# Attention inside a two-layer kernel: probabilities times values in three rounded passes, score rows through ScalarE and GpSimd

## Chip, cores and metric

One Trainium2 chip, one of its cores. The metric is the device time of one execution in microseconds (us), median of several runs.

## The reference

Two sequences of 1024 tokens, width 256. The kernel computes layer norm and attention with residual, a feed-forward layer with ternary weights, a Mamba layer and a feed-forward layer with 2:4 sparsity. Only attention matters here: 16 heads of 128 channels, causal, with a bias that grows linearly with the key position.

```python
q = (resid_pre @ Wq.T).reshape(b, s, H, DH)      # k, v likewise
scores = jnp.einsum('bqhd,bkhd->bhqk', q, k) / math.sqrt(DH)
scores = jnp.clip(scores, -1024.0, 1024.0)
scores = scores + _alibi_mask(H, s, s)[None]
attn = jax.nn.softmax(scores.astype(jnp.float32), axis=-1).astype(q.dtype)
z = jnp.einsum('bhqk,bkhd->bqhd', attn, v)
out = jnp.einsum('bqhd,ohd->bqo', z, Wo.reshape(d, H, DH))
```

## The kernel before

Attention runs as 16 bodies, one per pair of heads: 8 pairs for batch 0, then 8 for batch 1. The five engines have an instruction stream each, written out by hand, and meet at counting semaphores. An engine works its stream strictly in order, so the order in which a stream lists its steps is the order of the work.

Matrix products of fp32 accuracy are done in one of two ways. Most operands are split in a high part, rounded to the format fp32r, and a low part (the difference), and three passes high x high, high x low, low x high go into one accumulator (`passes`, line 265). The product of probabilities and values (`pe_product`, line 501) takes plain fp32 operands, `pt` and `v_sb`, in one instruction, which the trace shows as two records.

A score row k is 128 queries of one head against all keys up to them. Rows 0 to 7 are the first head of the pair, 8 to 15 the second; row k has (k mod 8 + 1) x 128 columns. In the text s12 is the product that computes row 12. A row goes this way: TensorE computes it into PSUM (`pe_scores`, 473); VectorE clips it into the tile `prob` in SBUF (`scores`, 1266), which frees the PSUM bank (`s_read`), then adds the causal bias and takes the row's minimum of the negated values in one custom instruction (1271, called the mask in this text); ScalarE takes the exponential and the row sum (`exps`, 892); VectorE the reciprocal (`recip`, 1277); GpSimd multiplies (`norm`, 1769). Then TensorE transposes 128 x 128 blocks of it.

The body has 24 slots. Slot n does the transposes of value block n (`pe_transposes`, up to four), then one larger job, `USES[n]`, then the product of block n-1. The larger jobs are in this order:

```python
USES = ("v1", "s12", "s13", "out1", "s8", "qk0", "s9", "s10", "s11", "qk1", "s14", "s15",
        "qk2", "s4", "s5", "qk3", "s0", "s1", "s2", "s3", "s6", "v0", "s7", "out0")
```

v1 and v0 project values (v0 those of the next pair), qk0 to qk3 project queries and keys of the next pair, out1 and out0 are output projections. Rows from s4 on in this list are already those of the next pair. The larger jobs use two double banks of PSUM in turn: a job in slot n needs that the result of slot n-2 has been read (`pe_free`, 418). A result is read by whoever evacuates it: scores by VectorE's clip, qk by ScalarE (high half) and then VectorE (low half), v by ScalarE (884) alone, out by VectorE's residual (1289). A transposed block is in one of two further banks and copied by ScalarE (`pts`, 899) into `pt`, which also has two buffers. The accumulators of the product are two more banks; they are read by ScalarE (`z`, 904) and VectorE (`z_rest`, 1282). Per pair there are 12 blocks of 512 columns, and 4 each of 384, 256 and 128.

Beside that, each body prepares a slice of the ternary weights on VectorE: `q_start` (1295), the four small steps `q_scales` (1319 to 1325), `q_signs` (1329, 1330) and the four bf16 steps `q_values` (1335 to 1342), 512 columns wide in batch 0, 256 in batch 1. GpSimd computes the low parts of the weights with subtractions from SBUF: `split_qk` (1747, for the pair after the next), `split_v` (1754) and `split_out` (1761), after ScalarE has rounded the high parts (855, 860, 866). Weights come by DMA from the SyncE queue.

VectorE's stream at the end of a body, with `ahead(k)` the clip and mask of row k of the next pair, is: `ahead(3)`, `next_recip(2)`, `ahead(6)`, `next_recip(3)`, `next_recip(6)`, `q_values()`, `ahead(7)`, `residual(out0)`.

Of the kernel before, what the change touches and what calls it, by code (L numbers as in the profile page):

```python
# [8 lines left out]
F32 = mybir.dt.float32  # L9
# [29 lines left out]
def program(nc, x_in, slopes_in, wqk_in, wv_in, wo_in, wgu0_in, wp0_in, win_in, wx_in, wdt_in,  # L39
# [3 lines left out]
    with ctx:  # L43
# [49 lines left out]
        v_sb = place(mem, "v_sb", [P, TILES, 2 * DH])  # L93
# [3 lines left out]
        pt = place(mem, "pt", [P, 2, BANK])  # L97
# [23 lines left out]
        def causal_row(k):  # L121
# [108 lines left out]
         o_added, wv_in_s) = (  # L230
# [4 lines left out]
                "wv_in"))  # L235
# [47 lines left out]
        USES = ("v1", "s12", "s13", "out1", "s8", "qk0", "s9", "s10", "s11", "qk1", "s14", "s15",  # L283
# [10 lines left out]
        def s_count(p, name, last=False):  # L294

            mine = [n for n in USES[:USES.index(name) + 1] if n[0] in "qs" and has(n, False, last)]
            return p * 20 + (FIRST_S + len(mine))

# [119 lines left out]
        def pe_free(pe, p, pos, begin=False, last=False):  # L418
# [4 lines left out]
            if prev == -2:  # L423
                pe.wait_ge(s_read, p * 20 + FIRST_S)
# [4 lines left out]
            elif USES[prev][0] in "qs":  # L429
                pe.wait_ge(s_read, s_count(p, USES[prev], last))  # L430
# [59 lines left out]

        def pe_transposes(pe, p, idx):
# [33 lines left out]
        def pe_attention(pe):  # L525
# [30 lines left out]
            for m in range(4):  # L556
                if m >= 2:
                    pe.wait_ge(s_read, m - 1)
                pe_qk(pe, 0, 0, m, m)
            for i, qt in enumerate(ROWS[:-1]):  # L560
                pe.wait_ge(s_read, 4 + i - 1)
# [3 lines left out]
            pe.wait_ge(s_read, 4 + 6)  # L565
            pe_v(pe, 0, 0, 0, 7)
            pe.wait_ge(s_read, 4 + 7)
# [10 lines left out]
            pe.wait_ge(s_read, s_count(LAST_PAIR, "s15", True))  # L578
# [271 lines left out]
        def act_attention(act):  # L850
# [30 lines left out]
            def v(p, m, pos):  # L881
                act.wait_ge(v_full, p * 2 + (m + 1))
                act.wait_ge(pv_done, p * 24 + (2 if m else 2 - 4))
                nc.scalar.activation(v_sb[:, 4 * m:4 * m + 4, :].rearrange("p t n -> p (t n)"),
                                     ps[:, s_bank(pos):s_bank(pos) + 2, :].rearrange("p a n -> p (a n)"),
                                     ACT.Copy).then_inc(v_read, 1)
# [8 lines left out]
            def pts(p, idx):  # L895
# [3 lines left out]
                nc.scalar.activation(pt[:, idx % 2, r0 * P:BANK], ps[:, 4 + idx % 2, r0 * P:BANK],  # L899
                                     ACT.Copy).then_inc(pt_read, 1)  # L900
# [6 lines left out]
            def body(p, b, begin=False, two_on=True, last=False):  # L907
# [8 lines left out]

                pts(p, 0)
                v(p, 1, 0)
                pts(p, 1)
                if not begin:  # L920
                    z(p - 1, 1, 1)
                pts(p, 2)
                exps(p, 12)
                q_magnitudes(p, b)
                pts(p, 3)
# [1008 lines left out]
```

## Time and profile before

| | |
|---|---|
| median of 3 runs | 1860.01 us (1858.03 to 1860.28) |
| profiled execution | 1858.39 us |
| its span | 1856.6 us |
| TensorE (PE) busy | 1714.1 us, 92% |
| VectorE (DVE) busy | 1415.1 us, 76% |
| ScalarE (ACT) busy | 1127.9 us, 61% |
| GpSimd (POOL) busy | 647.9 us, 35% |
| mean granted clock of TensorE | 0.976 |

The busy shares are means over stages with different limits. Attention lasts from the start to about 1006 us. A record of the timeline gives the start in us from the span's start, the duration, the engine, the line, the operation, the tile written and the tiles read. PE is TensorE's matmul; its records overlap, because matmuls are pipelined, so the time that a matmul takes is the distance from its start to the next one's. A bracket at the end of a line is idle time of that engine before the instruction, and what ended it.

### The profile page before, as it was taken

The numbers are of one execution on the slowest core, as the hardware profiler recorded it, in microseconds if no ns is written. First come the engines' busy times: TensorE is split into PE (matmuls) and PEld (weight loads), VectorE is DVE, ScalarE is ACT, GpSimd is POOL, SyncE is SP. The second block draws the span as 40 slices with busy tenths as digits, with TensorE's granted clock in tenths as the row PEclk, the third lists the DMA queues.
The fourth block names the chain that finished last, engine by engine and source line by source line (L and its number), as shares of the span: only waits on it lengthen the run. The fifth ranks groups of instructions, "written<-read, shape, count | busy, mean of one in ns | idle before, by whom it ended". The sixth has DMA issues, their size and how long they took to land. (4 is left out here: it accounts for less than half of the span.)

```text
span 1856.6 us, 30197 instructions
## 1 busy us (share of the span) xinstructions
PE 1714.1 (92%) x9232; PEld 1318.5 (71%) x9232; DVE 1415.1 (76%) x2239; ACT 1127.9 (61%) x2108; POOL 647.9 (35%) x517
## 2 busy tenths in 40 slices
PE   5999999999999999999998997899899798977997
PEld 3777778877877787778786886655457565556886
DVE  6777777777776777677764667788887788867997
ACT  3555555555555555565554554899877998943332
POOL 2332323322332233232221111089680397870000
PEclk9999999999999999999999998999999899998999
DMA  2000000000000000000001000123110232220000
GB/s 92 18 29 17 23 28 17 17 23 28 15 26 15 23 14 25 14 23 21 13 0 47 0 0 1 36 93 102 68 68 4 70 101 79 97 84 1 11 17 18
DMA packets 24139, 64.03 MB, mean 34 GB/s; under 512 B 2769, under 2 KB 7889, under 8 KB 23697
## 3 DMA queue, kind: packets, MB, share of 16 engines
q1 hardware_dynamic: 24080, 63.31, 10.2%
q8 instruction: 31, 0.51, 0.1%
q14 instruction: 28, 0.22, 0.0%
HBM read 60.94 MB, written 2.36 MB: 34 GB/s over the span
## 5 line engine op out<-in xcount | busy, mean ns | idle before, releaser
L1769 POOL TENSOR_SCALAR prob<-prob,rinv 128x640 f32<-128x640 f32 (+7 forms) x256 | 213.6, 835 | 674.3 <-DVE rinv L1277 673.1
L1846 POOL TENSOR_TENSOR m_h<-m_h,m_C 128x1024 f32<-128x1024 f32 x128 | 305.8, 2392 | 195.0 <-DVE m_h L1656 195.0
L1656 DVE TENSOR_TENSOR_SCAN m_h<-m_y,ps 128x1024 f32<-128x1024 f32 x128 | 291.5, 2284 | 53.9 <-PE ps L765 47.2
L892 ACT ACTIVATE prob<-prob,nmax 128x640 f32<-128x640 f32 (+7 forms) x256 | 198.4, 775 | 192.6 <-DVE nmax L1271 192.5
L508 PE MATMUL ps<-pt,v_sb 128*128 128x512 f32 (+3 forms) x768 | 310.4, 486 | 1.9 <-ACT pt L899 1.9
L899 ACT ACTIVATE pt<-ps 128x512 f32<-128x512 f32 (+3 forms) x384 | 186.1, 485 | 151.2 <-PE ps L498 150.1
L772 PE MATMUL ps<-m_h,ident 128*128 128x512 f32 x512 | 250.0, 612 | 11.3 <-POOL m_h L1846 11.3
L1271 DVE CUSTOM_DVE_ANT_0 prob<-prob,bias 128x640 f32<-128x640 f32 (+7 forms) x256 | 204.4, 799 | 44.8 <-issue 27.5
L498 PEld LDWEIGHTS ps<-ident,prob 128*128 128x128 f32 x1152 | 145.6, 140 | 116.6 <-issue 88.7
L1266 DVE TENSOR_SCALAR prob<-ps 128x640 f32<-128x640 f32 (+7 forms) x256 | 192.4, 751 | 42.4 <-PE ps L479 40.6
L1143 ACT ACTIVATE m_u<-m_uT,m_bT 128x256 f32<-128x256 f32 x512 | 211.1, 502 | 9.2 <-PE ps L765 9.1
L498 PE MATMUL ps<-ident,prob 128*128 128x128 f32 x1152 | 188.4, 273 | 0.0
L765 PEld LDWEIGHTS ps<-ident,m_u 128*128 128x128 f32 x1024 | 122.7, 144 | 90.6 <-issue 53.2
L479 PE MATMUL ps<-qk_hi 128*128 128x512 f32 (+2 forms) x384 | 153.8, 400 | 22.1 <-DVE qk_lo L1257 13.4
L765 PE MATMUL ps<-ident,m_u 128*128 128x128 f32 x1024 | 137.9, 278 | 19.9 <-DVE m_h L1656 8.4
L772 PEld LDWEIGHTS ps<-m_h,ident 128*128 128x128 f32 x512 | 89.6, 195 | 80.8 <-issue 63.9
L1149 ACT ACTIVATE m_y<-m_delta,negA 128x1024 f32<-128x1024 f32 x128 | 139.9, 1143 | 3.0 <-DVE m_h L1656 3.0
L508 PEld LDWEIGHTS ps<-pt,v_sb 128*128 128x128 f32 x768 | 131.7, 189 | 13.2 <-ACT pt L899 3.0
L479 PE MATMUL ps<-qk_hi,qk_lo 128*128 128x512 f32 (+2 forms) x384 | 132.0, 344 | 0.0
L479 PE MATMUL ps<-qk_lo,qk_hi 128*128 128x512 f32 (+2 forms) x384 | 131.7, 343 | 0.0
L1014 ACT ACTIVATE f_sg<-ps 128x512 f32<-128x512 f32 x64 | 38.1, 598 | 134.3 <-PE ps L618 134.3
L479 PEld LDWEIGHTS ps<-qk_hi 128*128 128x128 f32 x384 | 72.8, 190 | 38.3 <-DVE qk_lo L1257 17.3
(210 smaller groups left out, 3485.0 us busy)
## 6 DMA issues: line engine op xcount, KB each, us to landing
m_C<-bc_dram SPq DMA_DIRECT2D x64, 512.0 KB, 3.7
wqk_raw<-wqk_in SPq DMA_DIRECT2D x16, 512.0 KB, 3.3
wv_raw<-wv_in SPq DMA_DIRECT2D x16, 256.0 KB, 2.6
wo_raw<-wo_in SPq DMA_DIRECT2D x16, 256.0 KB, 2.9
x<-x_in SPq DMA_DIRECT2D x2, 1024.0 KB, 6.8
q_raw<-wgu_in SPq DMA_DIRECT2D x8, 256.0 KB, 2.7
raw<-wgu_in SPq DMA_DIRECT2D x1, 2048.0 KB, 7.9
out<-x SPq DMA_DIRECT2D x8, 256.0 KB, 2.1
```

The source lines that it names most:

```text
L479: mm = nc.tensor.matmul(flat[:, o + lo_c:o + hi_c], (qk_hi, qk_lo)[a][:, 2 * u, qt * P:(qt + 1) * P], (qk_hi, qk_lo)[w][:, 2 * u + 1, lo_c ...
L498: mm = nc.tensor.transpose(ps[:, 4 + idx % 2, r * P:(r + 1) * P], prob[:, at:at + P], ident[:, :])
L508: nc.tensor.matmul(ps[:, 6 + g, r0 * P:BANK], v_sb[:, j, u * DH:(u + 1) * DH], pt[:, idx % 2, r0 * P:BANK], start=(j == 0), stop=(j == 4 * ...
L765: mm = nc.tensor.transpose(ps[:, 4 + 2 * e + t // 4, (t % 4) * P:(t % 4 + 1) * P], m_uB[:, v % 2, t, e * P:(e + 1) * P], ident[:, :])
L772: mm = nc.tensor.matmul(ps[:, 2 * e + c, :], ident[:, :], m_h[:, 2 * (v % 2) + e, c * BANK:(c + 1) * BANK], start=begin, stop=end)
L892: nc.scalar.activation(prob[:, at:at + n], prob[:, at:at + n], ACT.Exp, bias=nmax[:, k:k + 1], scale=-1.0, accum_out=rsum[:, k:k + 1]).the ...
L1143: nc.scalar.activation(m_uB[:, v % 2, t, :], m_uT[:, half, t, :], ACT.Copy, scale=m_bT[:, t, bass.ds(it * RING + v, 1)]).then_inc(ub_done, 1)
L1266: nc.vector.tensor_scalar(tile, flat[:, o:o + n], CLIP, -CLIP, ALU.min, ALU.max).then_inc(s_read, 1)
L1271: nc.vector.tensor_tensor_reduce(out=tile, in0=tile, in1=bias[:, k // 8, S - n:S], scale=-1.0, scalar=BIG, op0=ALU.add, op1=ALU.min, accum ...
L1656: nc.vector.tensor_tensor_scan(m_h[:, 2 * (v % 2) + e, :], m_da[:, 2 * (v % 2) + e, :], drive(e), 0.0, ALU.mult, ALU.add).then_inc(scan_do ...
L1769: nc.gpsimd.tensor_scalar(prob[:, at:at + n], prob[:, at:at + n], rinv[:, k:k + 1], 1.0, ALU.mult, ALU.mult).then_inc(norm_done, 1)
L1846: nc.gpsimd.tensor_tensor(state, state, m_C[:, v, :], ALU.mult).then_inc(hc_done, 1)
```

## The change

The product of probabilities and values is done in three passes of rounded parts. For this `v_sb` is replaced by `v_hi` and `v_lo`, `pt` by `pt_hi` and `pt_lo`; ScalarE writes the high parts, VectorE the low parts, from the same PSUM bank, and the bank is free after VectorE's step (`pt_rest`, `v_rest`). For the block of 128 columns a tile of 256 columns is used, `edge_hi` and `edge_lo`, whose first half is zero, so the product is 256 columns wide.

The clip moves. ScalarE copies a score row from PSUM to `prob` (`copy`), which frees the bank (`s_copied`); GpSimd clips it in place in SBUF (`clip`, `s_clipped`); VectorE then does the mask alone. `USES` is reordered: qk0 moves from slot 5 to 8, qk1 from 9 to 10, and s9, s10, s11, s14 move accordingly. The streams of ScalarE, VectorE and GpSimd are written anew around that. The diff, cut to its core:

```diff
-        USES = ("v1", "s12", "s13", "out1", "s8", "qk0", "s9", "s10", "s11", "qk1", "s14", "s15",
+        USES = ("v1", "s12", "s13", "out1", "s8", "s9", "s10", "s11", "qk0", "s14", "qk1", "s15",
                 "qk2", "s4", "s5", "qk3", "s0", "s1", "s2", "s3", "s6", "v0", "s7", "out0")
@@ pe_product
-            pe.wait_ge(pt_read, p * 24 + (idx + 1 + 2))
+            c0 = min(r0, 2) * P
+            pe.wait_ge(pt_split, p * 24 + (idx + 1))
-            nc.tensor.matmul(ps[:, 6 + g, r0 * P:BANK], v_sb[:, j, u * DH:(u + 1) * DH],
-                             pt[:, idx % 2, r0 * P:BANK], start=(j == 0),
-                             stop=(j == 4 * g + 3)).then_inc(pv_done, 1)
+            for i, (a, w) in enumerate(((0, 0), (0, 1), (1, 0))):
+                if a:
+                    pe.wait_ge(pt_read, p * 24 + (idx + 1 + 2))
+                cols = (edge_hi, edge_lo)[a][:, :] if r0 == 3 else (pt_hi, pt_lo)[a][:, idx % 2, c0:BANK]
+                mm = nc.tensor.matmul(ps[:, 6 + g, c0:BANK], (v_hi, v_lo)[w][:, j, u * DH:(u + 1) * DH], cols,
+                                      start=(j == 0 and i == 0), stop=(j == 4 * g + 3 and i == 2))
+            mm.then_inc(pv_done, 1)
@@ ScalarE, new
+            def copy(p, k, count, pos):
...
+                nc.scalar.activation(prob[:, at:at + n], flat[:, o:o + n], ACT.Copy).then_inc(s_copied, 1)
@@ VectorE
-            def scores(p, k, count, pos):
-                nc.vector.tensor_scalar(tile, flat[:, o:o + n], CLIP, -CLIP, ALU.min, ALU.max).then_inc(s_read, 1)
+            def mask(p, k):
+                dve.wait_ge(s_clipped, row_count(p, k))
+            def pt_rest(p, idx):
+                nc.vector.tensor_tensor(turned(pt_lo, edge_lo, idx, r0), ps[:, 4 + idx % 2, r0 * P:BANK],
+                                        turned(pt_hi, edge_hi, idx, r0).bitcast(F32),
+                                        ALU.subtract).then_inc(pt_read, 1)
+            def v_rest(p, m, pos):
...
@@ GpSimd, new
+            def clip(p, k):
...
+                nc.gpsimd.tensor_scalar(prob[:, at:at + n], prob[:, at:at + n], CLIP, -CLIP,
+                                        ALU.min, ALU.max).then_inc(s_clipped, 1)
```

The new streams, where the prediction speaks of them (own rows and next rows are told apart by their numbers). ScalarE, from slot 4: `pts(4)`, `exps(13)`, `copy(8)`, `pts(5)`, `z(0,0)`, `copy(9)`, `split_out`, `pts(6)`, `exps(8)`, `copy(10)`, `pts(7)`, `exps(9)`, `copy(11)`, `pts(8)`, `exps(10)`, `qk(0)`; and from slot 20: `pts(20)`, `exps(2)`, `copy(6)`, `split_qk`, `pts(21)`, `exps(3)`, `v(0)`, `pts(22)`, `exps(6)`, `copy(7)`, `pts(23)`. VectorE, from block 2: `pt_rest(2)`, `mask(12)`, `pt_rest(3)`, `residual(out1)`, `mask(13)`, `pt_rest(4)`, `recip(12)`, `pt_rest(5)`, `recip(13)`, `z_rest(0,0)`, `mask(8)`, `pt_rest(6)`, `q_scales`, `mask(9)`, `pt_rest(7)`, `recip(8)`, `mask(10)`, `pt_rest(8)`, `recip(9)`, `mask(11)`, `qk(0)`; at the end: `pt_rest(20)`, `recip(1)`, `mask(3)`, `pt_rest(21)`, `recip(2)`, `q_values`, `mask(6)`, `v_rest(0)`, `pt_rest(22)`, `recip(3)`, `pt_rest(23)`, `recip(6)`, `residual(out0)`. GpSimd at the end: `clip(3)`, `norm(1)`, `clip(6)`, `norm(2)`, `split_qk`, `norm(3)`.

## Rows read from the trace of the kernel before

**Rows 1.** Busy time by stretch: PE, PEld, DVE, ACT, POOL, then granted clock, DMA.
```profile
300.00:360.40 60.40, 59.38 (x338) 47.58 (x337) 45.36 (x87) 34.22 (x71) 18.54 (x19) 1.00 0.07 21
```
**Rows 2.** Timeline of PE, the same place in two successive pairs.
```profile
299.06 0.49 PE L498 MATMUL ps<-ident,prob 128*128 128x128 f32 x3
...
359.48 0.49 PE L498 MATMUL ps<-ident,prob 128*128 128x128 f32 x3
```
**Rows 3.** Timeline of PE, the first pass of s1.
```profile
338.57 0.38 PE L479 MATMUL ps<-qk_hi 128*128 128x256 f32 x1 [0.86 <-DVE qk_lo L1257]
```
**Rows 4.** Timeline of PE, score passes and products of 256, 128 and 512 columns.
```profile
336.77 0.28 PE L479 MATMUL ps<-qk_hi,qk_lo 128*128 128x256 f32 x1
336.89 0.38 PE L508 MATMUL ps<-pt,v_sb 128*128 128x128 f32 x2
337.11 0.60 PE L498 MATMUL ps<-ident,prob 128*128 128x128 f32 x4
...
342.60 0.39 PE L479 MATMUL ps<-qk_hi,qk_lo 128*128 128x512 f32 x1
342.83 1.02 PE L508 MATMUL ps<-pt,v_sb 128*128 128x512 f32 x2
343.69 0.60 PE L498 MATMUL ps<-ident,prob 128*128 128x128 f32 x4
```
**Rows 5.** Groups by line (two of the page, then by shape): busy, mean ns.
```profile
L1769 POOL TENSOR_SCALAR prob<-prob,rinv 128x640 f32<-128x640 f32 (+7 forms) x256 | 213.6, 835 | 674.3 <-DVE rinv L1277 673.1
L1266 DVE TENSOR_SCALAR prob<-ps 128x640 f32<-128x640 f32 (+7 forms) x256 | 192.4, 751 | 42.4 <-PE ps L479 40.6
...
L1282 DVE TENSOR_TENSOR z_lo<-ps,z_hi 128x512 fp32r<-128x512 f32 x59 | 40.5, 687 | 50.7 <-ACT z_hi L904 50.7
L1257 DVE TENSOR_TENSOR qk_lo<-ps,qk_hi 128x1024 fp32r<-128x1024 f32 x30 | 36.7, 1224 | 21.6 <-ACT qk_hi L877 21.0
L1271 DVE CUSTOM_DVE_ANT_0 prob<-prob,bias 128x896 f32<-128x896 f32 x31 | 33.9, 1092 | 5.3 <-DVE prob L1266 5.3
...
L899 ACT ACTIVATE pt<-ps 128x512 f32<-128x512 f32 x180 | 106.2, 590 | 65.6 <-PE ps L498 65.4
L884 ACT ACTIVATE v_sb<-ps 128x1024 f32<-128x1024 f32 x30 | 30.8, 1026 | 32.8 <-PE ps L508 23.8 <-PE ps L457 9.0
L855 ACT ACTIVATE wqk_hi<-wqk_raw 128x1024 fp32r<-128x1024 f32 x15 | 15.7, 1045 | 0.0
```
**Rows 6.** Timeline, transposes on PE and copy on ACT; V's copy on ACT.
```profile
311.54 0.60 PE L498 MATMUL ps<-ident,prob 128*128 128x128 f32 x4
...
312.17 0.60 ACT L899 ACTIVATE pt<-ps 128x512 f32<-128x512 f32 x1 [0.27 <-PE ps L498]
...
299.26 1.03 ACT L884 ACTIVATE v_sb<-ps 128x1024 f32<-128x1024 f32 x1 [1.40 <-PE ps L508]
```
**Rows 7.** Timeline of DVE, third of the four group-scale steps.
```profile
310.07 1.20 DVE L1323 TENSOR_SCALAR q_scale<-q_scale 128x8 bf16<-128x8 bf16 x1
```
**Rows 8.** Timeline of POOL, then DVE: q_values, and one mask of 128 columns.
```profile
288.45 2.38 POOL L1747 TENSOR_TENSOR wqk_lo<-wqk_raw,wqk_hi 128x1024 fp32r<-128x1024 f32 x1
290.80 1.19 POOL L1769 TENSOR_SCALAR prob<-prob,rinv 128x896 f32<-128x896 f32 x1
...
288.82 2.29 DVE L1335 TENSOR_TENSOR q_abs<-q_abs,q_neg 128x512 bf16<-128x512 bf16 x1
291.14 1.39 DVE L1337 TENSOR_TENSOR q_abs<-q_abs,q_scale 128x512 bf16<-128x512 bf16 x1
292.56 0.42 DVE L1339 TENSOR_TENSOR q_abs<-q_abs,q_bf 128x512 bf16<-128x512 bf16 x1
...
307.97 0.89 DVE L1271 CUSTOM_DVE_ANT_0 prob<-prob,bias 128x128 f32<-128x128 f32 x1 [0.17 <-issue]
```
**Rows 9.** Timeline of PE after its longest idle time; busy times behind it.
```profile
46.58 0.80 PE L479 MATMUL ps<-qk_hi 128*128 128x512 f32 x1 [4.19 <-DVE prob L1266]
...
46.50:51.50 5.00, 4.92 (x18) 4.63 (x19) 4.13 (x10) 1.52 (x4) 1.06 (x2) 0.50 0.00 0
```

More of the change, by code:

```diff
@@ L92, in program @@
         qk_lo = place(mem, "qk_lo", [P, 4, S], F32R)
-        v_sb = place(mem, "v_sb", [P, TILES, 2 * DH])
+        v_hi = place(mem, "v_hi", [P, TILES, 2 * DH], F32R)
+        v_lo = place(mem, "v_lo", [P, TILES, 2 * DH], F32R)
         ramp = place(mem, "ramp", [P, S])
@@ L297, in s_count, with copy_count @@
             return p * 20 + (FIRST_S + len(mine))
+        def copy_count(p, name, last=False):
+            mine = [n for n in USES[:USES.index(name) + 1] if n[0] == "s" and has(n, False, last)]
+            return p * 16 + (8 + len(mine))
         def row_count(p, k):
@@ L915, in next_exps, with own_copy, next_copy @@
                         exps(p + 1, k)
+                def own_copy(k):
+                    copy(p, k, s_count(p, f"s{k}", last), USES.index(f"s{k}"))
+                def next_copy(k):
+                    if not last:
+                        copy(p + 1, k, s_count(p, f"s{k}"), USES.index(f"s{k}"))
                 pts(p, 0)
+                exps(p, 7)
                 v(p, 1, 0)
@@ L1349, in body, with next_mask @@
                 q_scales, q_signs, q_values = q_parts(p, b)
-                def own(k):
-                    scores(p, k, s_count(p, f"s{k}", last), USES.index(f"s{k}"))
-                def ahead(k):
+                def next_mask(k):
                     if not last:
-                        scores(p + 1, k, s_count(p, f"s{k}"), USES.index(f"s{k}"))
+                        mask(p + 1, k)
                 def next_recip(k):
@@ L1434, in dve_attention @@
             qk(0, 3, 3)
-            for i, k in enumerate(ROWS):
-                scores(0, k, 5 + i, i if i < 7 else 8)
+            for i, k in enumerate(ROWS[:-1]):
+                mask(0, k)
                 if i:
@@ L1772, in body, with next_clip, next_norm @@
             def body(p, two_on=True, last=False):
+                def next_clip(k):
+                    if not last:
+                        clip(p + 1, k)
+                def next_norm(k):
+                    if not last:
+                        norm(p + 1, k)
+                clip(p, 7)
+                norm(p, 6)
+                clip(p, 12)
                 norm(p, 7)
-                norm(p, 12)
-                norm(p, 13)
+                clip(p, 13)
                 if not last:
                     split_v(p + 1)
-                split_out(p)
-                for k in (8, 9, 10, 11, 14, 15):
-                    norm(p, k)
-                if not last:
-                    for k in (4, 5, 0, 1, 2, 3):
-                        norm(p + 1, k)
+                clip(p, 8)
+                norm(p, 12)
+                clip(p, 9)
+                norm(p, 13)
+                clip(p, 10)
+                split_out(p)
+                clip(p, 11)
+                norm(p, 8)
+                norm(p, 9)
+                norm(p, 10)
+                clip(p, 14)
+                norm(p, 11)
+                clip(p, 15)
+                norm(p, 14)
+                next_clip(4)
+                next_clip(5)
+                norm(p, 15)
+                next_clip(0)
+                next_norm(4)
+                next_clip(1)
+                next_norm(5)
+                next_clip(2)
+                next_norm(0)
+                next_clip(3)
+                next_norm(1)
+                next_clip(6)
+                next_norm(2)
                 if two_on:
                     split_qk(p + 2)
-                if not last:
-                    norm(p + 1, 6)
+                next_norm(3)
             pool_norm(pool, 0)
@@ L1792, in pool_attention @@
             pool_norm(pool, 1)
-            for k in ROWS[:-1]:
-                norm(0, k)
+            for i, k in enumerate(ROWS[:-1]):
+                clip(0, k)
+                if i > 1:
+                    norm(0, ROWS[i - 2])
+            norm(0, ROWS[5])
             split_qk(1)
```

208 lines of the change are left out of this document (140 added, 68 removed).

## The prediction

> **What bounds the kernel now.** I read the page first, then the busy times by stretch, then the timeline of TensorE (PE) over one head pair, then those of VectorE (DVE), ScalarE (ACT) and GpSimd (POOL) beside it. Between two stretches in which the same pair body repeats, PE is busy 59.38 of 60.40 us, DVE 45.36, ACT 34.22, POOL 18.54 [rows 1]. So PE sets the length of a pair, and the reader should see that its matmuls follow one another almost without an idle note. The same place of the body (three transposes of block 1) comes at 299.06 and at 359.48: one pair takes 60.42 us [rows 2]. The only stall of size is in front of scores s1: 0.86 us, until DVE has taken the low half of qk3 [rows 3]. There are 16 pairs, with a first one that starts at about 54 us and a last one without successor. Nothing outside attention is touched, so all of the change lies in these pairs.
>
> **What PE gains.** Durations of matmul records overlap; I use the distance of starts. A score pass of 512 columns takes 342.60 to 342.83 = 0.23 us, one of 256 takes 336.77 to 336.89 = 0.12; so 384 should take 0.18. A product in plain fp32 (two records) takes 342.83 to 343.69 = 0.86 with 512 columns and 336.89 to 337.11 = 0.22 with 128; so 0.65 and 0.43 for 384 and 256 [rows 4]. The new products are the same instruction form as the score passes, so three passes cost 0.69, 0.53, 0.36, and the 128-column ones, which are computed 256 wide, 0.36. A pair has 24 blocks: 12 of 512 (12 x -0.17 = -2.04), 4 of 384 (-0.48), 4 of 256 (-0.28), 4 of 128 (4 x +0.14 = +0.56). Sum: -2.24 us. Taking also today's stall out, to count it anew below: 60.42 - 0.86 - 2.24 = 57.3 us. That is the pair if nobody kept PE waiting.
>
> **What moves between the others.** Per pair, DVE loses 16 clips: 192.4 / 16 = 12.0 us [rows 5]. It gains 24 differences for the low halves of the probabilities, which are of z_lo's kind, 0.69 us for 512 columns [rows 5]; scaled down for the narrow ones I take 12 x 0.69, 4 x 0.55, 4 x 0.41, 4 x 0.28 = 13.2 us. Two differences of 1024 columns for V, at 1.22 as qk_lo [rows 5], make 2.4. So DVE has +3.6, some 49 us, in a pair of under 60. ACT gains 16 copies out of PSUM, 0.59 us for 512 and 1.03 for 1024 columns [rows 5]: about 10 us, to 44. POOL gains 16 clips; taken as the normalizations, 213.6 / 16 = 13.4 us, it comes to 32 [rows 5]. The clip is not in the trace in POOL's form: its lower bound is that of a free engine, nothing on the path, the upper one a mask delayed by every clip. By sums no engine passes PE. It is the order in the queues that decides, because the three buffers of PSUM that used to be freed by one engine are now freed by two in turn: the transposed block by ACT and then DVE, V by ACT and then DVE, and a score row goes ACT, POOL, DVE, ACT, DVE, POOL. PE issues in order, so each late release stops everything behind it.
>
> I walked each queue in the new order with these durations. A transposed block is copied from 0.63 us after its transposes start (311.54 to 312.17) and lasts 0.60 [rows 6]; its difference ends 0.7 us later.
>
> (a) s13 needs the bank of v1. ACT can start V's copy only after the product of block 23 (at 299.26, 0.20 behind the start of the slot after it [rows 2, 6]); copy 1.03, difference 1.22, so the bank is free at 2.5 in a slot chain where s13 could start at 2.04: +0.5.
> (b) In DVE's queue the mask of row 13 and the residual stand before block 4's difference, and the residual waits for the output projection. Residual 1.2, mask 0.96, difference 0.69: +0.3.
> (c) After block 6's difference DVE computes the four group scales, one of which takes 1.20 us for 8 columns beside a POOL subtraction [rows 7]; behind them wait mask 9, in ACT's queue exp 9, copy 11, block 8, exp 10, high half of qk0, then its low half on DVE, and qk1 on PE needs that bank. I get +0.9; if the scales ran undisturbed, nothing. Bounds 0 and 1.1.
> (d) s1 waits for the low half of qk3 as now (0.86), now behind mask 5, which may lose POOL to normalization 15: 0.7 to 1.4, taken 1.0.
>
> (e) The largest. The last slot's projection out0 takes the bank of v0, which today ACT frees at once; after the change it is freed by the difference of V on DVE, and that stands behind the four bf16 operations of q_values and mask 6. Count from the transposes of block 20. PE: transposes 0.36, s6 (six passes, 512 and 384 columns, and 0.1 to start) 1.33, product 0.69: 2.4. Then transposes 0.25, v0 (24 passes of 256 columns and 0.08) 2.96, product 0.69: 6.3; 0.13, s7 1.47, product 0.53: out0 could start at 8.45. ACT: s6 is there at 1.9, its copy ends at 2.85, the split of the next q and k weights (1.05 [rows 5]) at 3.9, block 21 at 4.4. DVE: difference 4.95, reciprocal 5.05, and now q_values. Today they run beside POOL's subtraction of those same weights (288.45, 2.38 us) and a normalization (1.19): the first takes 2.29, the second 1.39, the other two 0.42 each; they alternate with POOL, each waiting for the other's end [rows 8]. After the change POOL has again just those two in front, because the normalization of row 2 waits for the reciprocal ahead of q_values, and the subtraction is behind it. So again four times 0.42, 0.6 and 2.38 and the gaps: 4.75, to 9.8. Mask 6 (1.09 [rows 5]) to 10.9, difference of V (1.22) to 12.1. out0 is late by 12.1 - 8.45 = 3.65 us. If q_values met nobody (1.85) it would be 0.8. Until now the same lateness of DVE cost nothing, as only scores s7's clip, with two slots to spare, stood behind it.
>
> **The sum.** 57.3 + 0.5 + 0.3 + 0.9 + 1.0 + 3.65 = 63.65 us, 3.2 more than now. In the second batch the q operations are half as wide, which takes 0.6 from (e): +2.6. The weights' subtraction is there in pairs 0 to 13: 8 x 3.2 + 6 x 2.6 = 41 us. Pair 14 has no subtraction (+0.6); the last has short slots and a chain of two engines per block (within 1); the prologue loses DVE's clips and gets two hops (within 1.5). I take these at nothing together. The profiled execution took 1858.39 (span 1856.6); 1858.4 + 41 = 1899.4. The median of the runs shown, 1860.01, lies 1.6 above: 1901.
>
> **A rule that bears on it.** The 128-column mask at 307.97 took 0.89 us, where 896 columns take 1.09 [rows 5, 8]: it waited too. The Trainium skill, "SBUF — State Buffer", section "Who interferes with whom", says that a VectorE instruction with two SBUF inputs and a GpSimd instruction that reads SBUF shut each other out for the whole instruction. By that rule, which the row bears out, the 16 clips move from a place where they disturb nobody (DVE, from PSUM) to the one that blocks masks.
>
> **Rivals.**
> Fast pair: the chains overlap better than my walk says and q_values miss the subtraction, so PE waits 1.5 a pair in all: 58.8, 15 x -1.6 = -24, 1836. For it: no engine is full by sums, and rows and copies are issued up to two slots before they are needed. Against it: (a) and (e) are single chains that I can count. It decides at out0: under 0.8 of stall. Chance 0.30.
> Half of it: only (e) falls to 0.8 and the small ones stay: 57.3 + 2.7 + 0.8 = 60.8, +0.4 a pair, about 1866, from 1850 to 1872. Chance 0.08.
> Masks lose every race (slower side): POOL has a normalization ready behind most clips, and it starts at the clip's end, before DVE has seen the semaphore; masks 12, 5, 0, 1, 2, 3 then wait 0.5 to 1.1 each, and where no slack is left this adds 1.5 or more. In the same case a stall of 4 us may cost the clock: after PE's idle 4.19 us before 46.58 a score pass lasted 0.80 and the granted clock was 0.50, the 1.2 GHz level, from 46.5 to 51.5 [rows 9]. Together 65.5: 15 x 5 = +75, 1935. It decides from an out0 stall of about 4 us. Chance 0.12.
> The forecast (1880 to 1922) has 0.50.
>
> **Numbers.** What a measurement of this kernel can tell from no change is about 0.2%, 3.7 us. Faster: the fast rival and a part of the half one, 0.33; within it 0.04; slower 0.63. The range for 8 in 10 must take in most of the fast rival, since it holds 0.30, and the lower part of the slow one: 1828 to 1932. For the forecast alone 1880 to 1922.
>
> **What would show it.** Right if the distance of two equal places is 63 to 64.5 us; if three records of a 512-column product stand 0.23 apart; if PE's largest wait is that of the projection's first matmul for V's difference, 3 to 4 us in 14 pairs; if the first or second q_values operation lasts over 2.4 us beside POOL's subtraction. (c) is right if qk1's first matmul waits for qk0's low half. Wrong if the product passes come slower than 0.23 (then PE gains nothing), if q_values end within 2.5 us (then (e) is gone, and with it the sign), or if blocks' differences come late throughout, which would put waits of PE on the probabilities' low half in every slot.

## The result, and the profile after

The changed kernel takes 1903.38 us (median of 4 runs, 1899.78 to 1905.54), the kernel before 1859.76 in the runs beside it (1858.03 to 1860.28). The ratio is 1.0234, 95% interval 1.0214 to 1.0255: slower. The forecast was 1901, so sign and size came out; the terms behind it did so only in part, and the sections below say which.

The page of the changed kernel, the totals: busy us, share of the span (1903.6 us), instructions.

```profile
PE 1716.4 (90%) x9616; PEld 1388.9 (73%) x9616; DVE 1453.9 (76%) x2401; ACT 1252.9 (66%) x2364; POOL 853.9 (45%) x773
```

The groups that the change added or altered, also from the page.

```profile
L1866 POOL TENSOR_SCALAR prob<-prob 128x640 f32<-128x640 f32 (+7 forms) x256 | 188.3, 736 | 346.1 <-ACT prob L917 337.0
L1873 POOL TENSOR_SCALAR prob<-prob,rinv 128x640 f32<-128x640 f32 (+7 forms) x256 | 225.8, 882 | 151.0 <-DVE rinv L1346 135.9
...
L1333 DVE TENSOR_TENSOR pt_lo<-ps,pt_hi 128x512 fp32r<-128x512 f32 (+2 forms) x320 | 193.8, 606 | 95.1 <-ACT pt_hi L930 94.6
L1326 DVE CUSTOM_DVE_ANT_0 prob<-prob,bias 128x640 f32<-128x640 f32 (+7 forms) x256 | 229.0, 894 | 45.0 <-POOL prob L1866 32.8
```

The 256 clips on POOL cost 736 ns each, 11.8 us a pair (13.4 had been taken), and the normalizations rose from 835 [rows 5] to 882 ns. No engine is full, and PE, which was idle for 1.02 us of a pair [rows 1], now stands still for over four. By stretch of 63 us, in the first batch and in the second (PE, PEld, DVE, ACT, POOL, then granted clock, DMA):

```profile
300.00:363.00 63.00, 58.65 (x351) 51.16 (x350) 47.76 (x96) 40.67 (x85) 29.99 (x35) 0.97 0.06 21
663.00:726.00 63.00, 59.80 (x372) 52.37 (x371) 46.87 (x100) 43.14 (x89) 32.20 (x36) 1.00 0.06 19
```

Where PE waited during attention: engine and tile, what for; total us, times, longest.

```profile
PE ps L541 <- DVE v_lo L1339: 32.9, 14, 2.7
...
PE ps L490 <- DVE qk_lo L1316: 11.1, 15, 0.7
...
PE ps L490 <- DVE v_lo L1339: 6.1, 16, 2.1
PE ps L513 <- POOL prob L1873: 5.5, 17, 1.6
...
PE ps L455 <- DVE qk_lo L1313: 2.2, 7, 0.3
```

The largest is the one that the prediction named: the output projection waits for V's low half, 14 times. Its chain in one pair, PE first (the single transpose of slot 23, then out0's first matmul), then DVE (three of the four q_values steps, mask 6, V's difference):

```profile
304.63 0.27 PE L513 MATMUL ps<-ident,prob 128*128 128x128 f32 x1
307.64 0.39 PE L541 MATMUL ps<-wo_hi,z_hi 128*128 128x256 f32 x1 [2.75 <-DVE v_lo L1339]
```
```profile
301.35 0.98 DVE L1406 TENSOR_TENSOR q_abs<-q_abs,q_scale 128x512 bf16<-128x512 bf16 x1
302.36 2.50 DVE L1408 TENSOR_TENSOR q_abs<-q_abs,q_bf 128x512 bf16<-128x512 bf16 x1
305.02 0.42 DVE L1411 TENSOR_TENSOR q_out<-q_bf,q_abs 128x512 bf16 x1
305.36 1.08 DVE L1326 CUSTOM_DVE_ANT_0 prob<-prob,bias 128x896 f32<-128x896 f32 x1
...
306.37 1.22 DVE L1339 TENSOR_TENSOR v_lo<-ps,v_hi 128x1024 fp32r<-128x1024 f32 x1
```

The 2.50 us step, of a kind that takes 0.42 alone, ran beside this subtraction on POOL, and ended just behind it:

```profile
301.75 2.83 POOL L1844 TENSOR_TENSOR wqk_lo<-wqk_raw,wqk_hi 128x1024 fp32r<-128x1024 f32 x1
```

**Stage by stage.** DVE's residual of out0 marks the pairs. In the changed kernel, pairs 0, 8, 13 and 14:

```profile
119.11 1.23 DVE L1358 TENSOR_TENSOR x<-ps,x 128x1024 f32<-128x1024 f32 x1 [2.97 <-PE ps L541]
...
629.68 1.23 DVE L1358 TENSOR_TENSOR x<-ps,x 128x1024 f32<-128x1024 f32 x1 [1.73 <-PE ps L541]
...
938.01 1.23 DVE L1358 TENSOR_TENSOR x<-ps,x 128x1024 f32<-128x1024 f32 x1 [1.72 <-PE ps L541]
...
997.59 1.23 DVE L1358 TENSOR_TENSOR x<-ps,x 128x1024 f32<-128x1024 f32 x1 [1.92 <-PE ps L541]
```

The same four in the kernel before:

```profile
114.65 1.22 DVE L1289 TENSOR_TENSOR x<-ps,x 128x1024 f32<-128x1024 f32 x1
...
597.38 1.22 DVE L1289 TENSOR_TENSOR x<-ps,x 128x1024 f32<-128x1024 f32 x1
...
899.51 1.22 DVE L1289 TENSOR_TENSOR x<-ps,x 128x1024 f32<-128x1024 f32 x1
...
959.81 1.23 DVE L1289 TENSOR_TENSOR x<-ps,x 128x1024 f32<-128x1024 f32 x1 [0.99 <-PE ps L521]
```

Attention ends with the first transposes of the quantizer, PE's first matmul behind it, at 1053.52 after and at 1007.68 before. So the change costs 119.11 - 114.65 = 4.5 us up to pair 0, 510.57 - 482.73 = 27.8 over the next eight distances, 308.33 - 302.13 = 6.2 over five of the second batch, 59.58 - 60.30 = -0.7 in pair 14, and 55.93 - 47.87 = 8.1 in the last pair: 45.8 in all, of 47.0 that the two spans differ. The 1.2 us that are left lie behind attention, in code that the change does not touch.

### The profile page after: what moved, and what is told of

Its sections match the earlier page's. It is cut to its first block, busy times and chain, and to the rows that moved or that the text cites. A ratio compares the mean times of both kernels' runs of the same rounds, so it can differ in the third digit from the quotient of the medians.

```text
span 1903.6 us, 32214 instructions
## 1 busy us (share of the span) xinstructions
PE 1716.4 (90%) x9616; PEld 1388.9 (73%) x9616; DVE 1453.9 (76%) x2401; ACT 1252.9 (66%) x2364; POOL 853.9 (45%) x773
## 4 chain that ended last, share of the span: by engine, by line
PE 39%; DVE 21%; POOL 16%; issue 15%; ACT 8%; POOLq 1%; DMA 1%; DVEq 1%; ACTq 0%; SPq 0%
POOL m_h L1984 14%; PE ps L455 6%; PE ps L528 6%; PE ps L490 6%; PE ps L541 6%; PE ps L642 4%; PE ps L513 3%; PE ps L468 3%; PE ps L666 2%; DVE v_lo L1339 2%; ACT prob L917 2%; DVE prob L1326 1%; DVE q_abs L1408 1%; ACT pt_hi L930 1%; POOL prob L1866 1%
## 5 line engine op out<-in xcount | busy, mean ns | idle before, releaser
L1866 POOL TENSOR_SCALAR prob<-prob 128x640 f32<-128x640 f32 (+7 forms) x256 | 188.3, 736 | 346.1 <-ACT prob L917 337.0
L1873 POOL TENSOR_SCALAR prob<-prob,rinv 128x640 f32<-128x640 f32 (+7 forms) x256 | 225.8, 882 | 151.0 <-DVE rinv L1346 135.9
L1333 DVE TENSOR_TENSOR pt_lo<-ps,pt_hi 128x512 fp32r<-128x512 f32 (+2 forms) x320 | 193.8, 606 | 95.1 <-ACT pt_hi L930 94.6
L1326 DVE CUSTOM_DVE_ANT_0 prob<-prob,bias 128x640 f32<-128x640 f32 (+7 forms) x256 | 229.0, 894 | 45.0 <-POOL prob L1866 32.8
L930 ACT ACTIVATE pt_hi<-ps 128x512 fp32r<-128x512 f32 (+2 forms) x320 | 171.6, 537 | 101.5 <-PE ps L513 99.8
L917 ACT ACTIVATE prob<-ps 128x640 f32<-128x640 f32 (+7 forms) x256 | 166.6, 651 | 12.7 <-PE ps L490 12.1
L528 PE MATMUL ps<-pt_lo,v_hi 128*128 128x512 f32 (+2 forms) x320 | 120.6, 377 | 5.3 <-DVE pt_lo L1333 3.9
```

The lines of the kernel that those rows point to most:

```text
L528: mm = nc.tensor.matmul(ps[:, 6 + g, c0:BANK], (v_hi, v_lo)[w][:, j, u * DH:(u + 1) * DH], cols, start=(j == 0 and i == 0), stop=(j == 4 * ...
L917: nc.scalar.activation(prob[:, at:at + n], flat[:, o:o + n], ACT.Copy).then_inc(s_copied, 1)
L1326: nc.vector.tensor_tensor_reduce(out=tile, in0=tile, in1=bias[:, k // 8, S - n:S], scale=-1.0, scalar=BIG, op0=ALU.add, op1=ALU.min, accum ...
L1866: nc.gpsimd.tensor_scalar(prob[:, at:at + n], prob[:, at:at + n], CLIP, -CLIP, ALU.min, ALU.max).then_inc(s_clipped, 1)
L1873: nc.gpsimd.tensor_scalar(prob[:, at:at + n], prob[:, at:at + n], rinv[:, k:k + 1], 1.0, ALU.mult, ALU.mult).then_inc(norm_done, 1)
```

## The experiments

**The steps of q_values.** If they hold V's bank, moving them behind `next_recip(6)` takes out0's wait away. Nothing else is edited but a DVE wait that keeps them ahead of the next pair's `q_start`.

```diff
                 next_recip(2)
-                q_values()
                 next_mask(6)
...
                 next_recip(6)
+                q_values()
                 residual(p, b, 0, USES.index("out0"))
```

> The changed kernel with one step moved on VectorE: q_values behind the last reciprocal of the body, so that V's low half no longer waits for it. Theory (the changed kernel is slow mainly because V's low half stands behind q_values while GpSimd subtracts the weights): the projection's wait of 2.75 us in batch 0 and 1.9 in batch 1 goes, and with it the lower clock behind it; 8 x 3.0 + about 6 x 1.5 + 7 x 2.1 = 47 us less, about 1856 (1850 to 1866). Rival (the cost is in the two more hops of every row and block, and out0 only shows it): the wait reappears elsewhere, 1890 or more.

It took 1866.45 us (ratio 1.0038, 1.0023 to 1.0053): 37 us less than the changed kernel, and 0.5 above the range expected (1850 to 1866). The list of waits has no row of out0 for V any more. But another of V's waits grew, from 6.1 to 18.5 us:

```profile
PE ps L490 <- DVE v_lo L1339: 18.5, 16, 2.1
```

That is s13, which waited 0.26 us for v1's low half in the changed kernel and now waits 1.39. The rows that the late steps push back are the residual, mask 7 and, on ACT, exponential 7, and V's copy stands behind that one. So the theory held in place and cause, and (18.5 - 6.1) / 14 = 0.9 us a pair were handed on.

**The subtraction beside them.** The other way to the same end is to leave q_values and move POOL's subtraction behind the normalization of row 3.

```diff
-                if two_on:
-                    split_qk(p + 2)
                 next_norm(3)
+                if two_on:
+                    split_qk(p + 2)
```

> The changed kernel with one step moved on GpSimd: the subtraction of the next q and k weights behind normalization 3, so that q_values meet it no longer; VectorE's order is untouched. Theory (mutual exclusion of the two engines makes q_values long): the third of the four steps falls from 2.5 us to under 1, the wait before out0 from 2.75 to about 0.6 us in batch 0 and to 0 in batch 1, about 1866 (1858 to 1874). Rival (q_values is long whatever GpSimd does, or the subtraction only hits the next step in line): 1890 to 1903.

1874.12 us (1.0088, 1.0071 to 1.0105), 0.1 above the range expected (1858 to 1874). In DVE's timeline the same two steps as above, and the difference of V:

```profile
293.47 0.98 DVE L1406 TENSOR_TENSOR q_abs<-q_abs,q_scale 128x512 bf16<-128x512 bf16 x1
294.48 0.42 DVE L1408 TENSOR_TENSOR q_abs<-q_abs,q_bf 128x512 bf16<-128x512 bf16 x1
...
296.40 1.22 DVE L1339 TENSOR_TENSOR v_lo<-ps,v_hi 128x1024 fp32r<-128x1024 f32 x1
```

The step of 2.50 us takes 0.42. With the four steps in 2.45 us (293.03 to 295.48) instead of 4.53 (300.91 to 305.44), out0 still waits 0.67 in the first batch (8 times, 5.1 us in all) and not at all in the second. So 2.1 of the 2.75 us are the contention with POOL, and 0.7 the place of the steps in DVE's order. Here too a part was handed on: s13's wait for v1's low half rose from 0.26 to 1.16 us. The Trainium skill, "SBUF — State Buffer", section "Who interferes with whom", has it that a VectorE instruction with two SBUF inputs and a GpSimd instruction that reads SBUF exclude each other for the whole instruction; the pair 2.50 beside 2.83 and 0.42 without it agrees. By the same section a VectorE instruction with at most one SBUF input, outside the modes that use both ports, does not contend with GpSimd, and a difference, whose other input is in PSUM, is one: that of block 6 took 0.69 us (329.25) inside a POOL normalization (328.94 to 329.85) in the changed kernel, and that of block 4 the same 0.69 (325.66) with POOL idle. (V's difference took 1.22 in both kernels, but POOL stood idle beside it in both.)

**The product.** Here the product is the plain fp32 instruction again, on the high halves alone; the low halves are still computed, and nothing else differs.

```diff
-            for i, (a, w) in enumerate(((0, 0), (0, 1), (1, 0))):
...
+            nc.tensor.matmul(ps[:, 6 + g, r0 * P:BANK], v_hi[:, j, u * DH:(u + 1) * DH].bitcast(F32),
+                             turned(pt_hi, edge_hi, idx, r0).bitcast(F32), ...)
```

> The changed kernel with the product in one plain fp32 instruction on the rounded high halves instead of three passes; the low halves are still computed but left out of the product, so the result lacks them. All other steps and orders stay. Theory (three passes save TensorE 2.2 us a pair): each pair grows by 2.2 and gives back 0.6 where a wait was behind the product, so +1.6 x 16 = 26, about 1929 (1920 to 1938). Rival (the passes bring TensorE nothing, or the pair is set by VectorE's queue): 1898 to 1908.

1914.91 us (1.0301, 1.0284 to 1.0318): 11.5 more than the changed kernel and not 26. A miss. Out0's wait is shorter here, as a slower PE comes later to a bank that is free at the same time:

```profile
309.82 0.39 PE L536 MATMUL ps<-wo_hi,z_hi 128*128 128x256 f32 x1 [2.30 <-DVE v_lo L1334]
```

The next pair's out0 follows at 374.95, 65.1 us later, where the changed kernel has 64.4. Of the 2.2 us that the three passes save on PE, only 0.7 reach the time; most of the rest is waited away.

**Each half of the change by itself.** First the move alone: scores through ACT and POOL in the new order, with the plain product of the high halves and without any low half of V or the probabilities.

```diff
-            def pt_rest(p, idx):
-                nc.vector.tensor_tensor(turned(pt_lo, edge_lo, idx, r0), ps[:, 4 + idx % 2, r0 * P:BANK],
...
+            def pt_rest(p, idx):
+                pass
```

> One half of the change alone: scores copied by ScalarE and clipped by GpSimd, in the new order of all streams, but the product in one plain instruction on what ScalarE copied, no low halves of probabilities and V (left out of the result). Theory (the hops of the score rows cost little by themselves, VectorE's load does it): 59.5 us of matmuls and about 1 of waits a pair, as before the change, about 1860 (1850 to 1870). Rival (the hops cost): 1880 or more, with waits of TensorE for score copies or normalizations.

1865.42 us (1.0040, 1.0026 to 1.0054), as expected. A pair of the first batch takes 60.58 us, where the kernel before has 60.41; over the fourteen distances between the residuals of pair 0 and pair 14 the two differ by 2.6 us. The largest part of the loss is in the last pair, which with the way to the quantizer takes 53.80 us (960.74 to 1014.54) against 47.87 before. PE's two longest waits there:

```profile
989.15 1.12 PE L523 MATMUL ps<-pt_hi,v_hi 128*128 128x512 f32 x2 [2.24 <-ACT pt_hi L925]
...
993.63 0.70 PE L523 MATMUL ps<-pt_hi,v_hi 128*128 128x256 f32 x2 [2.38 <-ACT pt_hi L925]
```

Then the passes alone: DVE clips from PSUM as before, ACT copies no score row and POOL clips none, in the order of the changed kernel.

```diff
             def mask(p, k):
-                dve.wait_ge(s_clipped, row_count(p, k))
+                dve.wait_ge(s_full, full)
+                nc.vector.tensor_scalar(tile, flat[:, o:o + n], CLIP, -CLIP, ALU.min, ALU.max).then_inc(s_copied, 1)
+                dve.wait_ge(s_copied, row_count(p, k))
...
-                nc.gpsimd.tensor_scalar(prob[:, at:at + n], prob[:, at:at + n], CLIP, -CLIP,
-                                        ALU.min, ALU.max).then_inc(s_clipped, 1)
```

> The other half of the change alone: three passes with low halves on VectorE, but VectorE clips the scores out of PSUM right before each mask; ScalarE's copies and GpSimd's clips are gone. Orders otherwise as in the changed kernel. Theory (VectorE's load makes the time): its 47 us of a pair grow by 12.0 of clips and 16 x 0.17 of gaps to about 62, and with the waits before V's low half a pair takes 66 to 69, about 1970 (1930 to 2010). Rival (the hops of rows over ScalarE and GpSimd cost the time): 1870 to 1900, faster than the changed kernel.

2018.08 us (1.0867, 1.0847 to 1.0887), far above the 1970 expected and above the range (to 2010). Its stretch of one pair, and its largest wait in attention:

```profile
194.00:265.40 71.40, 61.38 (x362) 52.45 (x361) 56.21 (x113) 34.48 (x70) 17.59 (x19) 0.98 0.06 18
```
```profile
PE ps L490 <- DVE prob L1335: 94.1, 72, 3.8
```

DVE is busy 56 of 71 us, so it isn't full, but scores wait 72 times for its clip: a bank is freed where the mask stands in DVE's order, and this order puts differences ahead of it. So the move costs 7 us alone and the passes 159 alone; both together cost 44. In the order as written neither pays, and the move is what makes the passes bearable. The passes alone in an order made for them, such as that of the kernel before, were not run, so the 159 is the price of this order as much as of the passes.

**The four group scales** (c). Two experiments touch them. The first moves them by three blocks, and nothing else.

```diff
                 pt_rest(p, 6)
-                q_scales()
                 mask(p, 9)
...
                 pt_rest(p, 9)
+                q_scales()
                 recip(p, 10)
```

> The changed kernel with the group scales moved behind block 9's difference and nothing else. Theory as in the prediction (the scales delay qk0's low half, and qk1 waits 0.9 us for it in every pair): -13, about 1890. The profile of the changed kernel says less: that wait is 0.3 us, in batch 0 alone, so 8 x 0.4 = -3, about 1900. Rival (moved scales delay something later as much): 1903 and more.

1906.33 us (1.0258, 1.0241 to 1.0275): no gain. Pairs without a spell of low clock (explained below) took 63.0 and 63.1 us, against 62.94 in the changed kernel. The wait has moved from qk1, for qk0's low half (L1313), to qk2, for qk1's (L1316), and is no smaller:

```profile
340.55 0.74 PE L455 MATMUL ps<-a_xh,wqk_hi 128*128 128x512 f32 x2 [0.50 <-DVE qk_lo L1316]
```

**The narrow products.** The blocks of 128 columns are computed 256 wide; here they are 128 wide.

```diff
-            c0 = min(r0, 2) * P
+            c0 = r0 * P
...
-                cols = (edge_hi, edge_lo)[a][:, :] if r0 == 3 else ...
+                cols = (edge_hi, edge_lo)[a][:, P:2 * P] if r0 == 3 else ...
```

> The changed kernel with one size changed: the three passes of the 128-column blocks are 128 columns wide instead of 256 with a zero half. There are 4 such blocks in a pair. If a pass costs by its columns, 0.06 us instead of 0.12, it saves 3 x 0.06 x 4 = 0.7 us a pair, 1892. If it costs the same, 1903. If narrow passes are slow, say 0.23 each, it adds 3 x 0.11 x 4 = 1.3 us a pair, about 1924; that is what the zero half would be there for.

1901.76 us (1.0232, 1.0214 to 1.0249), the same as the changed kernel, and not the 1892 of a pass that costs by its columns. A pair without a spell of low clock took 62.85 us, against 62.94. PE's timeline shows why:

```profile
312.69 0.22 PE L528 MATMUL ps<-edge_hi,v_hi 128*128 128x128 f32 x1
312.75 0.28 PE L528 MATMUL ps<-edge_hi,v_lo 128*128 128x128 f32 x1
312.86 0.28 PE L528 MATMUL ps<-edge_lo,v_hi 128*128 128x128 f32 x1
```

The second pass starts 0.06 us after the first, the third 0.11 after the second, almost the 0.12 of 256 columns. The zero half costs nearly nothing.

**A better order.** If the waits are ones of order and not of load, a reordered kernel should beat the one before. This one has the late q_values; V's copy ahead of exponential 7 on ACT, with the reciprocal of row 7 behind `z_rest`; the late scales; qk3's low half ahead of the next bias; and normalization 15 ahead of clip 5.

```diff
                 pts(p, 0)
-                exps(p, 7)
                 v(p, 1, 0)
...
                 own_copy(12)
+                exps(p, 7)
...
                 next_mask(5)
+                next_qk(3)
+                pt_rest(p, 16)
                 if not last:
                     head_bias(p + 1, nb, 1)
-                next_qk(3)
-                pt_rest(p, 16)
...
-                next_clip(5)
                 norm(p, 15)
+                next_clip(5)
```

> The whole change with all steps kept and five moved in their queues: q_values as in e1_q_late; ScalarE copies V before exponential 7; the group scales behind block 9's difference; qk3's low half before the second bias, normalization 15 before clip 5. Theory (what is left of the loss are single waits of TensorE): from 61.0 and 60.1 us a pair in e1_q_late it falls by the 1.4 of s13, 0.4 of qk1 and about half of the 0.7 of s1, to some 58.7 and 58.5, about 1838 (1828 to 1848), faster than the kernel before. Rival (VectorE and ScalarE are so full that a moved step only pushes the next): 1855 to 1870.

1848.97 us (0.9945, 0.9929 to 0.9962), 0.55% faster than before, though 11 us above what was expected and 1 above the range; waits for the probabilities' low half (5.9 us, 15 times) and for qk1's low half (5.8, 14 times) were left. Without the moved scales:

> e6_reordered with the group scales back in their old place behind block 6's difference; the other moves stay. The lone move of the scales gave 1906 instead of 1903 and a wait of 0.5 us at qk2 in place of one of 0.3 at qk1. Theory (the moved scales only push qk1's low half and with it qk2): 14 x 0.5 - 8 x 0.4 = 3 to 4 us less than e6_reordered, about 1845 (1841 to 1849). Rival (nothing depends on their place): 1849 and a wait at qk1 as long as the one at qk2.

1849.2 us (0.9937, 0.9921 to 0.9954): the same time, where 1845 (1841 to 1849) had been expected. The waits only changed places: none is left for qk1's low half, but qk1 waits for qk0's again (2.5 us, 8 times), and those for the probabilities' low half grew from 5.9 to 7.4 us. The place of the scales is worth nothing here.

**Mask 13.** In DVE's stream of the changed kernel mask 13 stands behind the residual of out1, and the residual waits for PE:

```profile
323.64 1.22 DVE L1358 TENSOR_TENSOR x<-ps,x 128x1024 f32<-128x1024 f32 x1 [1.79 <-PE ps L541]
324.78 0.95 DVE L1326 CUSTOM_DVE_ANT_0 prob<-prob,bias 128x768 f32<-128x768 f32 x1
```

The clip of row 13 had been done since 321.05 + 1.27 = 322.32. The next experiment is the reordered kernel (scales kept) with the mask ahead of the residual.

```diff
+                mask(p, 13)
                 if not begin:
                     residual(p - 1, before, 1, USES.index("out1"))
-                mask(p, 13)
```

> e10_scales_kept with one more move on VectorE: mask 13 in front of the residual of out1 instead of behind it. Theory (the prediction's step b: mask 13 stands needlessly behind the wait for the projection, so that block 4's low half comes 0.3 us late): the wait of the product's third pass for it falls from 0.3 us to near 0 in 15 pairs, 4 us less than e10_scales_kept, about 1841 (1837 to 1845). Rival (the residual then comes a mask later and s9 waits for its bank): as e10_scales_kept or slower.

1833.78 us (0.9859, 0.9843 to 0.9876): 15 us off for one exchanged line, where 4 had been expected, so the range (1837 to 1845) was missed on the fast side; and 26 us (1.4%) faster than the kernel before. The wait of qk1 has no row left, and that for the probabilities' low half is down from 7.4 us (17 times) to that of the prologue and the last pair:

```profile
PE ps L490 <- DVE qk_lo L1316: 9.3, 15, 0.6
...
PE ps L528 <- DVE pt_lo L1333: 4.0, 3, 1.9
```

The same exchange in the changed kernel, and nothing else:

> The changed kernel with mask 13 in front of out1's residual and nothing else moved. Theory (mask 13 behind the residual is the cause of both the late low half of block 4 and of qk1's wait, which the prediction put down to the group scales; in e11_mask13 its move took 1.15 us off a pair of batch 0 and 0.85 off one of batch 1): the same here, 15 us less than the changed kernel, about 1888 (1883 to 1893), both waits gone. Rival (the gain in e11_mask13 came only because the body's end had been cleared; here the wait before out0 takes it back): 1898 to 1905.

1889.53 us (1.0162, 1.0141 to 1.0183): 13.9 us less than the changed kernel, as expected. Its four runs spread from 1885.04 to 1896.39, with mean granted clocks from 0.973 down to 0.962; pairs without a spell of low clock show the gain without that noise: 61.95 us (113.34 to 175.29) against 62.94 in the first batch, 60.86 against 61.67 in the second, 13 us over the fourteen. The wait at qk1 is gone there too, without any touch on the scales, no wait at qk2 has come in its place, and out0's is what it was (33.0 us, 14 times, longest 2.7).

## Why the prediction came out as it did

**What PE gains: right.** Three passes of 512 columns stand 0.23 us apart, as the prediction took them from the score passes:

```profile
293.69 0.40 PE L528 MATMUL ps<-pt_hi,v_hi 128*128 128x512 f32 x1
293.93 0.40 PE L528 MATMUL ps<-pt_hi,v_lo 128*128 128x512 f32 x1
294.16 0.40 PE L528 MATMUL ps<-pt_lo,v_hi 128*128 128x512 f32 x1
```

That this gain is worth its full size in a pair is another matter: the plain product showed 0.7 of 2.2 us. In the sum the gain was counted once in full and the waits on top, which is right as long as the waits are computed for the faster PE, and they were.

**(a) s13, right.** PE's timeline, the transposes of slot 2 and s13:

```profile
318.04 0.38 PE L513 MATMUL ps<-ident,prob 128*128 128x128 f32 x2
318.68 0.50 PE L490 MATMUL ps<-qk_hi 128*128 128x512 f32 x1 [0.26 <-DVE v_lo L1339]
```

The slot needs 0.13 to 0.14 us for its two transposes before a free s13 could start, and s13 starts 0.64 after them: 0.5 lost, as forecast. The bracket shows only 0.26, since the modelled end of the last transpose overlaps the wait; the distance of starts is the safer reading.

**(d) s1, right.** Forecast 1.0; the bracket says 0.74, and by starts it is 0.98 (0.36 of transposes between 290.22 and 291.56):

```profile
290.22 0.60 PE L513 MATMUL ps<-ident,prob 128*128 128x128 f32 x4
291.56 0.39 PE L490 MATMUL ps<-qk_hi 128*128 128x256 f32 x1 [0.74 <-DVE qk_lo L1316]
```

**(b) and (c), right in their sum, wrong in the cause.** Forecast 0.3 and 0.9. Measured in the first batch: block 4's third pass 0.3 late, and qk1 0.44 by starts (0.31 in its bracket). But from block 4's transposes to qk1 the changed kernel takes 13.52 us (323.71 to 337.23), and the reordered one with mask 13 ahead 12.58 (299.01 to 311.59), so 0.94 was lost between them, spread over blocks 4 and 5 and qk1. The step that failed is that of the scales, priced at 0.9 us a pair. They do last 1.30 us beside a POOL subtraction, as forecast, and they are in the chain of qk1, for with them moved qk1 no longer waits; but then qk2 waits 0.50, and no time is gained. Moving mask 13 alone, with the scales in place, took the whole away. The prediction had this mask in (b), as 0.96 us ahead of one difference. It did not follow it into ACT's queue, where exponential 13 waits for it, and behind that one the copy of s8, block 5's high half and all that (c) listed.

**(e) out0, right in place and mechanism, a little too large.** Forecast 3.65 and 3.05 us. By starts it is 3.0 (304.63 to 307.64, less the transpose) in the first batch and 2.1 in the second, for which the bracket says 1.87. The q_values took 4.45 us where 4.75 was taken, with the long step third and not first, and the rest of the shortfall is in the DVE work ahead of them, which ended at 300.91 and so earlier than in the walk.

**The clock, left out of the sum: it stood only in a rival.** The prediction tied a loss of clock to a stall of about 4 us, since that was the nearest row [rows 9]. Windows of 6 us behind three of the stalls: after one of 2.75 us, after one of 2.73, and after one of 1.87 (columns as in rows 1).

```profile
308.00:314.00 6.00, 6.00 (x41) 6.00 (x40) 2.05 (x4) 1.30 (x3) 2.76 (x3) 0.72 0.00 0
...
436.00:442.00 6.00, 5.57 (x47) 5.57 (x48) 3.54 (x9) 2.09 (x6) 2.77 (x3) 1.00 0.00 0
...
625.00:631.00 6.00, 4.49 (x38) 4.49 (x39) 3.53 (x9) 2.73 (x5) 2.76 (x3) 1.00 0.01 3
```

A mean of 0.72 over 6 us is a spell at 0.50, the 1.2 GHz level, in the middle of 2.4 GHz. Seven of the eight stalls of 2.6 to 2.75 us in the first batch have it behind them; the one at 436.43 has not, and none of the six of 1.87 in the second has. Other executions show that this is no sharp line. In the three kernels whose waits before out0 are the same (the late scales, the narrow products, mask 13 alone), 2, 3 and 1 of the eight long stops were spared, and 1, 1 and 3 of the six of 1.87 to 1.89 had a spell behind them, such as this one of mask 13 alone (the stop ends at 620.02):

```profile
620.40:626.40 6.00, 6.00 (x41) 6.00 (x40) 2.07 (x4) 1.27 (x3) 2.74 (x3) 0.72 0.00 0
```

In the changed kernel, the pair with the spared stall gives the price: out0 comes at 372.03, 436.43 and 499.37, so 64.40 us with a spell and 62.94 without. That is 1.46 us a pair, 10 us in seven. With the plain product it is the same: 65.1 us with a spell, and 63.63 (246.19 to 309.82) behind the one stall that was spared. With the late q_values and with the late subtraction, where the stall is gone or 0.67, the clock stays at 1.00.

**One wait not foreseen:** block 16's transposes wait for normalization 15, which stands behind clip 5 on POOL (0.38 us a pair by starts, 17 times, 5.5 us in all).

**The pair, then:** 3.0 + 1.46 + 0.5 + 0.94 + 1.0 + 0.4, with 0.16 at s5, are 7.4 of the 64.4 us in the first batch (forecast 63.65), and 57.0 are left for the matmuls (the walk had 57.3). Without the clock, qk1's wait and 0.9 of out0's it is 61.7 in the second batch (forecast 63.0). So waits alone make a pair of 62.94, 0.7 less than forecast, and a term that the sum did not have brings it to 0.75 more. Of the signs named beforehand, the distance of 63 to 64.5 us held in the first batch only; out0's wait was the largest, in 14 pairs, but 3.0 and 2.1 us by starts and not 3 to 4; and the q_values step of over 2.4 us was the third, not one of the first two.

**The ends, wrong.** The last pair was taken at nothing, "within 1"; it costs 8.1 us. It has no projections for a next pair, so its slots are short, and PE has little to hide a late step behind. Two of its waits:

```profile
1018.30 0.50 PE L528 MATMUL ps<-pt_lo,v_hi 128*128 128x512 f32 x1 [1.60 <-DVE pt_lo L1333]
...
1027.77 0.50 PE L528 MATMUL ps<-pt_hi,v_hi 128*128 128x512 f32 x1 [1.64 <-ACT pt_hi L930]
```

Behind them the granted clock is 0.54 from 1030 to 1040, while that stage of the kernel before had 1.00 throughout; the longest stop there is 1.64 us, among shorter ones. The prediction named a chain of two engines per block and gave it no price. But that chain is the smaller part: the kernel with the move alone, which has no low halves at all, already loses 5.9 of the 8.1 us there (53.80 against 47.87). Its wait at 989.15 and the one at 1027.77 here are the same: the block's copy on ACT stands behind the exponential of an 896-column row, for whose mask ACT had stood idle 2.45 us in both kernels (1.14 in the kernel before), and the mask had waited for the clip, one of the new hops of a score row. So the total of 41 us against 45.8 is right partly by compensation: the second batch and pair 14 came out 8 us cheaper than forecast (6.2 - 0.7 against 5 x 2.6 + 0.6), the last pair 8 dearer; the first batch and what leads to it 4 dearer.

**The rivals.** The fast pair needed an out0 stall under 0.8, and the half one only that; both fell with the 2.75. The slow one's races were lost in part: mask 12 took 1.64 us and mask 5 1.84 beside clips and normalizations, and by shape the mask of 768 columns rose from a mean of 957 to 1370 ns, that of 640 from 826 to 1210 and that of 896 from 1092 to 1312; but masks of up to 512 columns are no longer than before, and over all 256 the mean rose only from 799 to 894. What the longer masks cost in time no run shows by itself. Its second half, the clock, was real at a lower price and from a shorter stall. That a better order of the same change would be faster than before (1833.8, run above) was in no rival; it bears on the change, not on the forecast.

## What to carry to other kernels

When a bank that one engine freed is now freed by two in turn, look up what stands in front of the second step in its queue: here 4.5 us of quantizer work with slack to spare became the wait that set the time, and exchanging two lines (a ready mask behind a residual that waits for PE) was worth 14 us. Follow a late step into the queue of the engine that waits for it, not only along its own. And price the last body, which has no successor's work to hide behind, by itself.

## What the runs showed of the hardware

- A single full stop of PE of 2.6 to 2.75 us in a pair of 64 was followed by a spell at 1.2 GHz in 7 cases of 8, which cost another 1.46 us; in the kernel with the plain product stops of 2.18 to 2.31 us were, too, in 7 of 8 (each with 0.72 to 0.77 over 6 us behind it, the spared one with 1.00). The six stops of 1.87 us in the second batch had 1.00 behind them, but over the four kernels with the same waits 5 of 24 stops of 1.87 to 1.89 us had a spell behind them and 25 of 32 of 2.6 to 2.75; with the passes alone it was 3 of 6 of 2.0 us. What decides the single case the runs don't settle.
- VectorE and GpSimd, both with ready work that excludes the other, took turns: the first q step ended at 301.32, POOL's normalization at 301.79, the second step at 302.33, the subtraction at 304.58, the third step at 304.86. In this one sequence whoever waited came next, so the long subtraction delayed one step of the four.
- Of three passes of 128 columns in the rounded format the second starts 0.06 us after the first and the third 0.11 after the second; with 256 columns it is 0.12 throughout, with 384 0.18, with 512 0.23.
